# GNN kernel: relative node numbers spread over partitions by TensorE, one-hots by ScalarE, one slots stage, picks in bf16

## The reference

```python
xl = (x @ Wl + bl).reshape(n, H, C)          # H = 4 heads, C = 128
xr = (x @ Wr + br).reshape(n, H, C)
s = leaky_relu(xl[src] + xr[dst], 0.2)
e = einsum('ehc,hc->eh', s, att)             # one score per edge and head
alpha = softmax of e over the edges of one dst
out = segment_sum(alpha[:, :, None] * xl[src], dst, n).mean(axis=1) + b
```

## Time and profile before

| what | value |
|---|---|
| profiled execution | 3452.38 us |
| its span | 3450.4 us |
| PE busy | 2609.4 us, 76% |
| VectorE busy | 2286.9 us, 66% |
| ACT busy | 1001.6 us, 29% |
| POOL busy | 817.2 us, 24% |
| window slots | about 15.0 to 78.5 us |
| slots and message slots | 551.4 to 662.2 us |
| scores of the two layers | about 763 to 1410 and 1891 to 2546 us |

### The profile page before, as it was taken

How to read it: one execution, slowest core, us unless ns; L and a number is a source line. 1 busy time by engine, 2 the same in 40 slices (tenths; PEclk the granted TensorE clock), 3 DMA queues, 4 the chain that set the end, 5 groups by cost and what they waited for, 6 DMA issues and landing times. The chain is left out here.

```text
span 3450.4 us, 53250 instructions
## 1 busy us (share of the span) xinstructions
PE 2609.4 (76%) x12797; PEld 1556.3 (45%) x12797; DVE 2286.9 (66%) x10981; ACT 1001.6 (29%) x2296; POOL 817.2 (24%) x858
## 2 busy tenths in 40 slices
PE   3775695287888888379857788888855995698998
PEld 1443583144444444246643444444433665244444
DVE  4666664577888888954497688888895447333323
ACT  0776692050000000135525000000012553233333
POOL 0000000016666666200000666666630000000000
PEclk8999797589999999689988899999977998898999
DMA  0000600038888888255423888888834552500000
GB/s 23 2 1 3 252 1 14 24 131 275 283 284 284 283 280 283 64 127 149 134 45 114 272 286 283 280 285 278 283 108 98 152 149 57 236 1 7 16 17 19
DMA packets 396226, 507.40 MB, mean 147 GB/s; under 512 B 29059, under 2 KB 331908, under 8 KB 394532
## 3 DMA queue, kind: packets, MB, share of 16 engines
q0 software_dynamic: 66560, 274.39, 23.6%
q1 hardware_dynamic: 329380, 229.61, 23.0%
HBM read 409.28 MB, written 94.61 MB: 146 GB/s over the span
## 5 line engine op out<-in xcount | busy, mean ns | idle before, releaser
L914 POOL DMA_INDIRECT rows<-row_table,idx x832 | 792.1, 952 | 797.5 <-POOLq L132 324.2
L965 PE MATMUL z_ps<-xr,hot_ta 128*128 x2496 | 693.4, 387 | 212.5 <-DVE rows L1008 183.1
L976 PE MATMUL z_ps<-rows,ident 128*128 128x256 f32 x1664 | 573.9, 427 | 5.0 <-issue 3.5
L2069 PE MATMUL dense_ps<-cnt,h 128*128 128x512 f32 (+1 forms) x1050 | 417.3, 555 | 86.9 <-ACT cnt L2027 83.3
L965 PEld LDWEIGHTS z_ps<-xr,hot_ta 128*128 128x128 bf16 x2496 | 243.8, 98 | 512.3 <-issue 396.9
L1008 DVE SCALAR_TENSOR_TENSOR rows<-rows,att_all 128x128 f32<-128x128 f32 x1664 | 423.4, 290 | 37.1 <-remote 23.6
L1034 DVE TENSOR_TENSOR rows<-z_ps,rows 128x256 f32<-128x256 f32 x832 | 348.2, 418 | 109.7 <-PE z_ps L976 73.0
L1008 DVE SCALAR_TENSOR_TENSOR rows<-z_ps,att_all 128x128 f32<-128x128 f32 x1664 | 410.2, 281 | 12.8 <-issue 12.5
L1343 PE MATMUL acc_m<-xr,hot_m 128*128 x1984 | 342.1, 295 | 69.6 <-issue 29.8
L1343 PEld LDWEIGHTS acc_m<-xr,hot_m 128*128 128x128 f32 x1984 | 270.9, 193 | 184.2 <-issue 181.1
L2069 PEld LDWEIGHTS dense_ps<-cnt,h 128*128 128x128 f32 x1050 | 189.6, 193 | 295.4 <-issue 198.5
(11 more groups left out here) (399 smaller groups left out, 3226.4 us busy)
## 6 DMA issues: line engine op xcount, KB each, us to landing
xr<-kept_rows SPq DMA_DIRECT2D x124, 512.0 KB
kept_rows<-rows SPq DMA_DIRECT2D x416, 128.0 KB
spread_a<-rel_rows SPq DMA_DIRECT2D x208, 128.0 KB
counts_line<-counts SPq DMA_DIRECT2D x1, 19550.0 KB
counts<-counts_line SPq DMA_DIRECT2D x6, 3200.0 KB
rows<-row_table,idx POOLq DMA_INDIRECT x832
row_table<-xl_ring SPq DMA_DIRECT2D x50, 258.0 KB
rows<-row_table SPq DMA_DIRECT2D x32, 320.0 KB
```

Of the source, the lines that this page charges most:

```text
L914: nc.gpsimd.indirect_dma_start(out=rows[:, u, :], out_offset=None, in_=table, in_offset=bass.IndirectOffsetOnAxis(ap=c.idx[:, n:n + 1], ax ...
L965: nc.tensor.matmul(ps[:, n % Z, :], hot, tile[:, m, 0:HC], start=m == 0, stop=False, skip_group_check=True)
L976: nc.tensor.matmul(ps[:, n % Z, HALF_C:HC], c.ident[:, :], rows[:, n % ROWS, HALF_C:HC], start=False, stop=True, skip_group_check=True).th ...
L2069: last = nc.tensor.matmul(ps[:, SUM, q % 2, 0:size * W_NODES], h[:, k, :], cnt[:, n % BUFS, 0:size * W_NODES], start=k == 0, stop=k == NOD ...
```

## The change

1. `gat_scores`: the spread load and VectorE's comparison go. PE writes the half's relative numbers to all partitions with four bf16 matmuls of 128 columns into one PSUM bank, out of `c.rel_row`, which stays in SBUF; the left operand is a column of the identity, broadcast. ACT makes Abs(spread - partition) and then Relu(1 - that), which is 1 where they are equal and 0 elsewhere. PE issues the spread of half k + 2 ahead of slot 1 of half k; ACT makes the one-hot at the first slot of a half. z_ps has 5 banks instead of 6. `rel_rows` in DRAM is gone.
2. `make_slots` and `message_slots` are one phase. dst is loaded once (SP), src on ACT's queue; both tables are counted, picked and spread one behind the other, and the message table's chain stands on VectorE between the store of dst_line and its use.
3. Picks are bf16 there and in `window_slots`. What a pick moves is split in a bf16 value and a bf16 rest, so there are two matmuls for it (one where 8 bits are enough); values constant along the free axis are broadcast instead of copied.

The core of the diff:

```diff
 def gat_scores(...):
-    Z = 6
+    Z = 5
             @block.sync
-                def load(k):
-                    sp.dma_start(spread[:, k % HOTS, :], bass.AP(rel_rows.tensor, k * HALF * P,
-                                                                 [[0, P], [1, HALF * P]]))\
-                      .then_inc(s["spread"][k % HOTS], 16)
-                    if n % HALF == 0 and k + HOTS < HALVES:
-                        sp.wait_ge(s["hot_t"], k + 1)
-                        load(k + HOTS)
             @block.tensor
+                def spread_half(k):
+                    if k > 0:
+                        pe.wait_ge(s["away"], k)
+                    for n in range(k * HALF, k * HALF + HALF):
+                        r = n % SB
+                        last = nc.tensor.matmul(spread[:, n % HALF * P:(n % HALF + 1) * P],
+                                                row_pick[:, r:r + 1].to_broadcast([SB, P]), c.rel_row[:, n // SB, :],
+                                                start=True, stop=True)
+                    last.then_inc(s["spread"], 1)
                 for n in range(SLOTS):
+                    if n % HALF == 1 and k + HOTS - 1 < HALVES:
+                        spread_half(k + HOTS - 1)
             @block.scalar
+                def one_hot(k):
+                    act.wait_ge(s["spread"], k + 1)
+                    nc.scalar.activation(away[:, k % 2, :], spread[:, :], ACT.Abs, bias=minus_part[:, 0:1])\
+                      .then_inc(s["away"], 1)
+                    if k >= HOTS:
+                        act.wait_ge(s["z"], (k - HOTS + 1) * HALF)
+                    act.wait_ge(s["away"], k + 1)
+                    nc.scalar.activation(hot_t[:, k % HOTS, :], away[:, k % 2, :], ACT.Relu, bias=c.ones[:, 0:1],
+                                         scale=-1.0).then_inc(s["hot_t"], 1)
                     for u in range(0, GROUP, 2):
+                        if u % HALF == 0 and n // HALF + HOTS - 1 < HALVES:
+                            one_hot(n // HALF + HOTS - 1)
             @block.vector
-                    nc.vector.tensor_scalar(hot_t[:, k % HOTS, :], spread[:, k % HOTS, :], c.part[:, 0:1], None,
-                                            ALU.is_equal).then_inc(s["hot_t"], 1)
-                    if n % HALF == 2 and n // HALF + HOTS - 1 < HALVES:
-                        one_hot(n // HALF + HOTS - 1)

 def make_slots(nc, c, src, dst, dst_line):      # one phase for both tables
+            @block.scalar
+                act.wait_ge(s["pads"], 2)
+                edges(act, src, src_i, s["src_in"])
-                sp.dma_start(rel_rows[0:SLOTS * P].rearrange("(b r e) -> r b e", r=SB, e=P),
-                             rel_row[:, :, :]).then_inc(s["rows_out"], 16)
-                sp.dma_start(rel_rows[SLOTS * P:(SLOTS + WIDE) * P].rearrange("(r e) -> r e", e=P),
-                             rel_row[0:WIDE, 0, :]).then_inc(s["rows_out"], 16)
+                link(nc.vector.tensor_copy(both_1[:, :, :, :], both_f[:, :, :, :]))
+                nc.vector.tensor_tensor(out=both_2[:, :, :, :], in0=both_f[:, :, :, :], in1=both_1[:, :, :, :],
+                                        op=ALU.subtract).then_inc(s["parts"], 1)
-                    nc.vector.tensor_scalar(shift_w[:, b, :], c.ones[:, :], shift[:, b:b + 1], None, ALU.mult)
-                    for h in range(H):
-                        link(nc.vector.tensor_copy(any_break[:, k, :, h], through[:, :, edge]))
+                    nc.vector.tensor_copy(any_break[:, k, :, :],
+                                          through[:, :, edge:edge + 1].to_broadcast([SB, SLOT_BLOCKS, H]))\
+                      .then_inc(s["broken"], 1)
             @block.tensor
+                spread(SRC, SLOTS, (lambda b: both_1[:, 1, b, :], lambda b: both_2[:, 1, b, :]))
+                spread(DST, SLOTS, (lambda b: both_1[:, 0, b, :], lambda b: both_2[:, 0, b, :]))
+                spread(TIL, SLOTS, (lambda b: wide(starts_1[:, 1, b:b + 1]), lambda b: wide(starts_2[:, 1, b:b + 1])))
+                spread(USE, SLOTS, (lambda b: ones_b[:, :],)).then_inc(s["slots"], 1)
+                pe.wait_ge(s["m_picked"], EDGE_BLOCKS)
...
 def window_slots(...):
-                    nc.vector.tensor_scalar(shift_w[:, b, :], c.ones[:, :], shift[:, b:b + 1], None, ALU.mult)
+                for half in range(2):
+                    spread(WIN, half, (lambda b: shift_1[:, b:b + 1].to_broadcast([P, P]),
+                                       lambda b: shift_2[:, b:b + 1].to_broadcast([P, P])))
+                    spread(DST, half, (lambda b: dst_1[:, b, :], lambda b: dst_2[:, b, :]))
+                    spread(LO, half, (lambda b: lo_b[:, b, :],))
+                    last = spread(HI, half, (lambda b: hi_b[:, b, :],))
```

More of the change, by code:

```diff
@@ L132, in phase, with make_slots @@
     nc.all_engine_barrier()
-def make_slots(nc, c, src, dst, rel_rows, dst_line):
+def make_slots(nc, c, src, dst, dst_line):
     with ExitStack() as ctx:
@@ L170, in make_slots @@
         any_break = sb("any_break", [SB, 2, SLOT_BLOCKS, H])
-        ps = ctx.enter_context(nc.psum_tensor(fresh(nc, "slot_ps"), [P, BANKS * BANK], F32))
-        PRE, SRC, DST, TIL, USE, REL, ROW, BRK = (k * BANK for k in range(BANKS))
-        with phase(nc, pads=0, loads=0, iotas=0, vec=0, pe=0, row_parts=0, rows_out=0, rows_back=0) as (block, s):
+        ends_i = sb("m_ends_i", [P, 3, EDGE_BLOCKS], I32)
+        ends = sb("m_ends", [P, 3, EDGE_BLOCKS])
+        m_slots = sb("m_n_slots", [P, EDGE_BLOCKS])
@@ L233, in _ @@
                 for b in range(1, EDGE_BLOCKS):
[L234 to L240, removed]
@@ new lines, in _ @@
+                for b in range(EDGE_BLOCKS):
+                    m_link(nc.vector.tensor_scalar(m_from_first[:, b, :], slot_no[:, :], m_first[:, b:b + 1], None,
+                                                   ALU.is_ge))
+                    nc.vector.scalar_tensor_tensor(out=m_pick[:, b, :], in0=slot_no[:, :], scalar=m_end[:, b:b + 1],
+                                                   in1=m_from_first[:, b, :], op0=ALU.is_lt, op1=ALU.mult)\
+                      .then_inc(s["m_picked"], 1)
@@ L314, in _ @@
-                last.then_inc(s["pe"], 1)
-                pe.wait_ge(s["vec"], V + 2 * (2 + SLOT_BLOCKS + H + 1))
-                for k, at in ((0, BRK), (1, PRE)):
+                for sem, bank, n, before, done in (("counted", BEFORE, n_slots, n_before, "before"),
+                                                   ("m_counted", M_BEFORE, m_slots, m_before, "m_before")):
+                    pe.wait_ge(s[sem], EDGE_BLOCKS - 1)
+                    to = ps[:, bank, 0:EDGE_BLOCKS]
+                    nc.tensor.matmul(to, later[:, :], n[:, :], start=True, stop=False)
+                    nc.tensor.matmul(to, c.ones[:, :], before[:, :], start=False, stop=True).then_inc(s[done], 1)
@@ new lines, in spread @@
+                def spread(bank, n, parts):
+                    for b in range(EDGE_BLOCKS):
+                        for k, left in enumerate(parts):
+                            last = nc.tensor.matmul(ps[:, bank, 0:n], left(b), (pick if n == SLOTS else m_pick)[:, b, :],
+                                                    start=b == 0 and k == 0,
+                                                    stop=b == EDGE_BLOCKS - 1 and k == len(parts) - 1)
+                    return last
+                pe.wait_ge(s["parts"], 1)
@@ L521, in norm_relu @@
+                    last.then_inc(s["breaks"], 1)
 def norm_relu(nc, c, x, out, gain=None, shift=None, dot=None):
@@ L875, in relu_scores, with gat_scores @@
     return last
-def gat_scores(nc, c, g, rel_rows, table, kept):
-    Z = 6
+def gat_scores(nc, c, g, table, kept):
+    Z = 5
     ROWS = 14
@@ L898, in gat_scores @@
         rows = ctx.enter_context(nc.sbuf_tensor(fresh(nc, "rows"), [P, ROWS, ROW], F32))
-        with phase(nc, used=0, gathered=ROWS, spread=HOTS, hot_t=0, z=0, sides=0, side=0, lin=0, added=0, summed=0,
+        with phase(nc, used=0, gathered=ROWS, picks=0, minus=0, spread=0, away=0, hot_t=0, z=0, sides=0, side=0, lin=0, added=0, summed=0,
                    vec=0, kept=ROWS // 2) as (block, s):
@@ L2267, in graph_layers @@
         c.slot_brk = sb("slot_brk", [H, 2, SLOTS], within=early)
-        make_slots(nc, c, src, dst, rel_rows, dst_line)
-        message_slots(nc, c, dst)
+        make_slots(nc, c, src, dst, dst_line)
         norm_relu(nc, c, x, h)
```

517 lines of the change are left out of this document (249 added, 268 removed).

## The result

On the chip of the result the changed kernel takes 3421.78 us (4 runs, 3420.88 to 3422.83) against 3446.59 for the one before: ratio 0.9928, 95% interval 0.991 to 0.9945. It is 25 us or 0.7% shorter, clear of the noise, where 152 us were forecast; 3293 and the range up to 3350 were both missed.

What follows compares the result with a forecast made beforehand. VectorE was taken to set the pace in the scores, with 0.216 us a slot of stalls. Terms -12.6, -50 and -90 gave -152.6 from 3452.4, so 3299.8 profiled and 3293 as median; own range 3262 to 3315, wider 3195 to 3350.

Steps and rivals of the forecast that it cites:

- Window slots, -12.6: Window slots: bf16 matmuls replacing f32 ones save 13.3 us, VectorE work adds 0.7; net -12.6 us, bounds -10 and -14.
- Slots stages, -50: Two slots stages merged: fewer loads, hidden waits and cheaper broadcasts save 50 us, bounds -43 and -54.
- One-hots off VectorE, -27 us a layer: Scores stage: 104 one-hots of 0.26 us leave VectorE, 27 us a layer or 0.065 a slot.
- PE's and ScalarE's new work: Scores stage: four matmuls add 0.10 us a slot, making PE's floor 1.29; ScalarE's two activations take 0.7 each, nothing waits.
- I let a fifth of the stalls go: Scores stage: of VectorE's 0.216 us a slot of stalls, 0.045 goes with the spread loads, leaving a slot of 1.408.
- the scores' term: Scores of both layers: the slot falls from 1.518 to 1.408 us, saving 45 us a layer, -90 in all.
- The stall-free end: End of layer 1's scores: 17 slots at 1.283 us each without stalls, after the last spread load; cited for rival B.
- rival B: Scores: stalls go altogether with spread loads and one-hots, PE binds at 1.30 us a slot; -244 in all, 3201; chance 0.3.
- Rival C: Scores: stalls stay whole, coming from gathers or kept-row stores; 3329, or 3383 if they grow; chance 0.26.
- the milder form: Rival C with stalls unchanged: only the one-hots' 27 us a layer go, -117 in all, 3329.
- the harder one: Rival C with stalls growing to fill the scores' gain: -63 in all, 3383.
- The rule of the Trainium skill: Scores: VectorE's one-hot tensor_scalar and GpSimd lock each other out (rival B); L1008's two SBUF inputs contend with GpSimd (Rival C).

Runs made afterwards that it cites:

- e2: The changed kernel with only the first 14 of 416 gathers a layer; 3148.45 us, ratio 0.9672, on a chip without stalls.
- e12: The changed kernel as it is, run again on a chip without stalls; 3148.88 us, ratio 0.967 to the kernel before.
- e4: e1 with five z banks instead of six; 3412.23 us, ratio 0.9815 to the kernel before, on a chip with stalls.
- e2c: The changed kernel with only the first 14 gathers of a layer, on a chip with stalls; 3161.93 us, ratio 0.9117 to the kernel before.
- e3b: The changed kernel without stores of kept rows in the scores (filled once elsewhere), on a chip with stalls; 3534.95 us, ratio 1.0192.
- e6: The changed kernel with VectorE making the one-hots from PE's spread, no ScalarE activations; 3460.37 us, ratio 0.9957, on a chip with stalls.
- e1: The changed kernel with the scores stage of the kernel before put back; 3408.65 us, ratio 0.9815, on a chip with stalls.
- e10c: e1 with one-hots, spread loads and tile loads for eight slots at a time, on a chip with stalls; 3404.51 us, ratio 0.9816.
- e5: e1 with the one-hots made by ScalarE from the loaded spread; 3417.09 us, ratio 0.9831, on a chip with stalls.
- e7: e1 with four small ScalarE copies added per two slots; 3195.19 us, ratio 0.9815, on a chip without stalls.
- e11: e1 with one 512-column ScalarE copy added per two slots; 3195.36 us, ratio 0.9816, on a chip without stalls.
- e10: e1 with one-hots, spread loads and tile loads for eight slots at a time; 3174.04 us, ratio 0.9749, on a chip without stalls.
- e13: The changed kernel once more, on another chip without stalls; 3150.22 us, ratio 0.9687 to the kernel before.
- e3: The changed kernel without stores of kept rows in the scores (filled once elsewhere); 3244.68 us, ratio 0.997, on a chip without stalls.

## Why the prediction was wrong, step by step

- **Window slots, -12.6.** Right: -12. The bf16 matmuls took 10.34 us of VectorE's waiting where 23.02 were the earlier trace rows; 9.6 was the estimate.
- **Slots stages, -50.** Right in its mechanism, -54, at its bound. The waits left on the path are these, where 3.5 us for the broadcasts alone had been left standing:
```profile
544.06 0.17 DVE L276 TENSOR_SCALAR span_i<-both_i 128x8 int32<-128x8 int32 x1 [1.67 <-DMA both_i<-in_dst]
546.11 0.17 DVE L290 COPY m_ends_i<-both_i 128x4 int32<-128x4 int32 x1 [0.57 <-DMA m_ends_i<-in_dst]
562.63 0.59 DVE L346 TENSOR_TENSOR tile_f<-slot_ps,slot_no 128x416 f32<-128x416 f32 x1 [0.95 <-PE slot_ps L484]
```
  The wait for the read back of dst_line is gone, as forecast, behind the message table's chain.
- **One-hots off VectorE, -27 us a layer.** The work did go, from 1.33 to 1.27 us busy a slot. On chips without stalls the scores fell by 23 us against the old scores (552 to 529), short of 27 because GpSimd's 1.25 us stopped it; without the gathers they are at 527 (e2), with PE and VectorE both busy over 99%. On the chip of the result none of it arrived.
- **PE's and ScalarE's new work.** An Abs takes 0.69 and a Relu 0.72 us (0.7 forecast). PE's floor of 1.29 was too high, since the four matmuls were mis-sized. From the first one's start to their last end is 0.39 us, near the forecast 0.40, but the next matmul starts 0.22 us after the first of them (e12, PE, start and duration):
```profile
1001.18 0.81 PE L972 MATMUL z_ps<-xr,hot_ta 128*128 x3
...
1002.37 0.81 PE L972 MATMUL z_ps<-xr,hot_ta 128*128 x3
...
1003.57 0.39 PE L947 MATMUL spread_ps<-rel_row,row_pick 104*128 104x128 bf16 x4
1003.79 0.81 PE L972 MATMUL z_ps<-xr,hot_ta 128*128 x3
```
  They start 0.057 us apart and add 0.22/4 = 0.056 us a slot and not 0.10, near the lower bound of 0.05 by columns: their weight loads run beside the matmuls before them, from 1003.35 on, and don't set the pace. PE's floor is 1.19 + 0.056 = 1.246, and e2, in which no GpSimd is in the way, runs at 1.247. The bank cost nothing (e4).
- **The step that failed: "I let a fifth of the stalls go".** It took the stalls for something that the spread loads might share in, gave 0.045 of 0.216 us a slot, and made the scores' term -90 us with a slot of 1.408. The slot took 1.57, and the term came out at +31 (18 + 13). The runs show stalls that belong to the gathers (e2c), are for the most part signals that arrive late, and don't care for spread loads or stores (e3b has neither). And they grew: idle time a slot is 0.19 before, 0.20 in e6, 0.21 in e1 and 0.22 in e10c, but 0.27 in e5, 0.30 in the changed kernel and 0.31 in e3b. That VectorE has less to do in these three isn't shown as the reason, since they are also the three in which ScalarE makes the one-hots. The signs were in the earlier trace rows: the stall lay between a multiply and the read of its own accumulator, where there is no spread load to wait for. The stall-free end, rival B's support, had both ends in it: the last spread load at 1382.02 and the last gather at 1394.55, behind which most of it lies; the loads got the credit that was the gathers'.
- **Rival C** ("grow to fill the gain") names what happened, but its 3383 let them take back the gain and no more; they took 16 us a layer beyond it. The range ended at 3350 with a chance given to C of 0.26: the milder form was counted in and the harder one only by half.
- The profile's "DVE rows L1034 <- PE z_ps" was read as a share of waiting for PE. In all 39 gaps over 0.2 us before an L1034 in the steady part, PE had started that slot's last matmul 6.1 to 8.4 us earlier. 35 of them (30.3 us) end with a recorded raise of PE's semaphore: the profile is right on the signal, and the work had been done. They were stalls too.
- The rule of the Trainium skill, "SBUF — State Buffer", section "Who interferes with whom", on VectorE and GpSimd locking each other out stood beside rival B and gave C its L1008. As a cause of these stalls it doesn't hold alone: the same multiplies and the same gathers run side by side without a stall on three chips (e12: 381 gathers in 475 us, VectorE busy 99.3%), and ScalarE stood still as well, of which the same section says that it never waits on anyone. Both were waiting for semaphores.

What stays open: what it is in a chip, or beside it, that makes the engines' signals late while gathers run (three sets of runs out of six met it, that of the result included, with before at 3446.6, 3475.6 and 3466.5 us; the others had 3254 to 3255), whether recording the trace has a part in it, and why the changed kernel has more of it. Untried were gathers of the same number but fewer bytes, which would tell a gather's issue from its data, the changed kernel beside e1 on one chip that stalls, and e7 or e11 there, which would tell ScalarE's part.

No version is best on both kinds. Without stalls the changed scores are (0.967 to 0.969, e10 0.975 to 0.977); with stalls the old ones seem to be (0.9815 for e1 and 0.9816 for e10, against 0.9928, each on another chip). Either way the new preparation brings 60 to 67 us (e7 and e1 against before).

## What to carry to other kernels

Idle time of the bounding engine that its own instructions and waits don't explain is not slack that a lighter program will fill: find out what it belongs to (take the gathers out, in one run) before giving an edit its work back as time. Where a wait ends late, compare when the semaphore was raised with when the work behind it ended: here that told a slow engine from a slow signal. The price of a short matmul is the distance to the next start, and not its duration. Measure on more than one chip before a verdict of under some per cent: the same pair of kernels gave 0.993 on one and 0.967 on another. A long stage of serial waits on VectorE is the safe part: merging two of them and putting one's chain behind the other's round trip gave what the sum said, and the merged stage takes 56 to 58 us in every trace looked at (result, e1, e7, e12, e13).

## What was not expected of the hardware

- The kernel before takes 3254 to 3255 us in three sets of runs and 3446 to 3476 in three others. Nearly all of the difference is in the scores, where GpSimd gathers.
- VectorE stalls of up to 2.9 us, some 130 a layer of over 0.15 us in the changed kernel, beside gathers. Most of their time is late semaphores: PE's spread has its semaphore raised 2.1 us (median) after its end, where it is 0.01 us on the chips without stalls and in e2c, without gathers. Even an instruction that waits for nothing can stand in such a stretch.
- At the start of a layer's scores the fourth slot comes 9 to 13 us behind the third on the chips that stall, 1.2 to 2.2 on the others. In e2c, with 14 gathers left, it is still 9.
- GpSimd issues gathers of 128 rows no faster than one in 1.25 us, with the DMA engines at 97% (e12) or 86% (e3).
- Four bf16 matmuls of 128 columns, each with other weights, start 0.057 us apart at the full clock.
